# Attention with a two-of-eight expert layer on one core: the attention phase's order, counted in ticks, is replaced by one that is played through

## The chip, the cores and the metric

One NeuronCore of one Trainium2 chip. The time is device microseconds (us) of one execution of the whole program, taken as the median of repeated runs. TensorE is written PE here, VectorE DVE, ScalarE ACT, GpSimd POOL and SyncE SP, as in the profile.

## What is computed

The input is x of 4 batches of 1024 tokens with 512 features, in float32. The output is x + attention(layernorm(x)) + experts(layernorm(x)):

```python
xn = _layernorm(x, axis=-1)
# attention: 16 heads of 32, causal, with a linear distance bias per head
scores = einsum('bhqd,bhkd->bhqk', q, k) / sqrt(D)
scores = where(causal, -inf, scores) + alibi_bias
out = softmax(scores) @ v, then @ Wo.T + bo
# experts: softmax over 8 gates, the two highest per token, weights renormalised
act = silu(g) * u          # g, u = xn @ w1 (352 each)
expert_out = act @ w2
```

## The kernel before

The program has three stretches. A short prologue normalises batch 0 and splits the weights of the attention into float16 pairs (a high and a low half; each product is three float16 products, `PASS`). The **attention phase** follows, and then the **expert phase**, in which 71 slots of 128 gathered tokens each go through one expert's two products and are added to the output by indirect DMAs.

The attention phase is cut into 16 groups (4 batches by 4 groups of 4 heads). A group has 40 **units**, so `NU` is 640. Unit u is one head and one pair of key tiles against two query tiles: PE makes the scores (step `score`, L1271 with L1273, or with L1275 and L1276 on the diagonal) in one of two half banks of PSUM, and ACT takes their exponential (step `exp`, L1875). `score` u waits for `exp` u-2, whose half bank it takes. Four units are a **quad** t, whose exponentials lie in one of three buffers (`PT`). Behind a quad come `add` (POOL sums halves of the exponentials, L1999, L2006, L2010, L2015), `acc` (DVE adds to the row sums, L1656), `pv` (PE, probabilities by values, L1289). `exp` of quad t waits for `pv` and `add` of quad t-3. Behind the quads of a quarter q of the queries come `rsum` (PE, L1299), `osb` (ACT copies the result out of PSUM, L1906), `fold`, `rcp` and `unfold` (a DMA, a reciprocal at L1660 and a DMA back), `bc` (PE, L1309), `a32` (DVE, L1664), `aTh` (ACT, L1855 and L1856) and `aT` (POOL, L2021). `osb` waits for the `aT` that last read the same buffer.

Other work is mixed in between the units:
- for the next group, the q, k and v projections (`qk` L1210, `v` L1227), the copies `qk32` (ACT, L1822), `qkh` (ACT, L1832), `qkl` (POOL, L1984), `vsb` (ACT, L1845) and `stack`, three DMAs for each of 4 heads on SP's queue (L1059);
- for the next group, upper bounds of the scores: 38 pieces `pre` on PE (L1243, L1248), each followed by `mx` on DVE (L1643), then `join`, `mtr` (PE, L1258), `mcp` (ACT, L1882) and the DMA `mrow` (SP, L1076);
- the output projection `o` of a finished batch (PE, L1321, three thirds of four matmuls for each of 8 tiles) with `y` (DVE, L1671) and `ostore`;
- the layer norm of the next batch: `bn` (DVE), `newton` (13 small POOL operations from L1966 on), `xn` (DVE, L1553), `xnh` (ACT, L1778), `xnl` (POOL, L1975), `xtp` (PE, L1165) and `xt` (ACT, L1791);
- the largest magnitude of the experts' weights (`wmax`) and their split into halves (`wsh` ACT L1917, `wsl` DVE L1705, `wstore`), and, from unit 454 on, the routing (`route`, mostly small DVE operations; `slots`, `places`, `lists`).

Four banks of PSUM (`PB`) are lent to `pre`, `qk`, `v`, `o`, `mtr`, `bc` and `xtp` (`borrow`, `give`), and are handed back by the step that empties them: for `pre` that is `mx`.

The order of all this is made by `plan()`, which runs once when the program is built and writes one list of steps. Every engine walks through the list and issues its own steps in that order, each with its waits; so on an engine a step whose wait isn't over holds up all that stand behind it. In the kernel before, `plan()` counts in **ticks**: one tick is one unit. In tick u it writes `score(u)` and `exp(u)`, then whatever is due at fixed distances in ticks (`add` 1 tick behind its quad, `pv` 2, `unfold` 4 and `bc` 9 behind `osb`), up to two `pre` from unit -27 of their group on, one piece of each running job of a list (`pace`), and as much of the projections (`fill`) as a credit allows, which grows by 0.62 of matmul time in each tick. The time that a step takes on DVE, ACT or POOL isn't in this reckoning.

## Time and profile before

| | us |
|---|---|
| median of 3 runs | 1599.39 (1597.41 to 1603.39) |
| the profiled execution, its own time | 1597.73 |
| its span, first to last instruction | 1595.9 |
| first score matmul starts | 74.3 |
| last score matmul starts | 1117.5 |

The profiled execution took 1.83 us more than its span, and 1.66 us less than the median of the runs. The span has the prologue up to 74, the attention phase from 74 to 1118, a turn from 1118 to about 1171 in which the last quarter is finished and the experts' weights are loaded, and the expert phase. On the page, each engine has its busy share; the granted clock of PE stands beside each stretch, 1.00 being 2.4 GHz. A matmul's duration in the trace is longer than what it holds PE for, since matmuls overlap: 0.27 us is shown for one of 256 columns, and the next starts 0.11 us after it.

### The profile page before, as it was taken

To read this page: it belongs to the slowest core of one execution; us is meant where nothing else is said; L and a number is where in the kernel's file an instruction comes from. 1 tells how busy PE (TensorE), PEld (TensorE's weight loads), DVE (VectorE), ACT (ScalarE), POOL (GpSimd) and SP (SyncE) were. 2 spreads that over 40 slices of the span, in tenths; PEclk is the share of its full clock that TensorE was granted. 3 is DMA by queue.
4 is the path that set the end of the run, shared out by engine and by line. 5 is a ranking of instruction groups with operands and counts; after the bars stand their busy time and mean duration, and the time that the engine had idled before them with its cause. 6 is when DMAs were issued, how large, how long until landed. Compare 5 with 4: busy or idle time off the path is not lost.

```text
span 1595.9 us, 32893 instructions
## 1 busy us (share of the span) xinstructions
PE 1419.4 (89%) x12219; PEld 838.9 (53%) x12219; DVE 947.9 (59%) x1742; ACT 799.1 (50%) x1403; POOL 948.4 (59%) x756
## 2 busy tenths in 40 slices
PE   4689978989997999998899899877789999999995
PEld 2355545544554555555455456543356656566663
DVE  8567776666687657766669976672243333333332
ACT  5255666646677675766676455456122222222221
POOL 4134576645577655656675567676217777777774
PEclk9899998989999999998899999997899999999998
DMA  6245433435533536333244210233877778888973
GB/s 245 61 128 148 124 94 102 123 90 148 156 94 97 152 101 197 103 117 94 88 110 126 83 43 13 68 115 106 288 180 126 136 130 131 131 137 148 132 137 47
DMA packets 189156, 193.51 MB, mean 121 GB/s; under 512 B 104883, under 2 KB 138931, under 8 KB 188876
## 3 DMA queue, kind: packets, MB, share of 16 engines
q1 hardware_dynamic: 160492, 152.01, 35.7%
q0 software_dynamic: 26128, 37.24, 13.9%
q8 instruction: 105, 1.72, 0.5%
q10 hardware_dynamic: 2384, 2.16, 0.4%
q14 instruction: 47, 0.39, 0.1%
HBM read 92.88 MB, written 53.74 MB: 92 GB/s over the span
## 4 chain that ended last, share of the span: by engine, by line
PE 55%; DVE 13%; POOL 11%; DMA 7%; issue 6%; ACT 4%; SPq 4%; ACTq 0%; POOLq 0%; DVEq 0%
PE S L1359 15%; PE O L1390 4%; PE M L1390 4%; DVE arena L1643 4%; PE T L1210 3%; DVE arena L1656 3%; DMA arena<-arena 3%; PE M L1289 3%; PE S L1210 3%; PE S L1243 2%; SPq L1059 2%; PE T L1243 2%; PE S L1271 2%; PE O L1289 2%; POOL arena L2006 2%
## 5 line engine op out<-in xcount | busy, mean ns | idle before, releaser
L1875 ACT ACTIVATE arena<-S,psl 128x512 f32<-128x512 f32 (+1 forms) x640 | 399.5, 641 | 256.0 <-PE S L1273 152.2
L2064 POOL DMA_INDIRECT out<-arena x142 | 222.1, 1564 | 104.7 <-issue 40.5
L1359 PE MATMUL S<-arena 128*128 x1704 | 267.1, 313 | 5.2 <-issue 5.2
L1643 DVE TENSOR_REDUCE arena<-S 128x1 f32<-128x512 f32 (+3 forms) x311 | 202.0, 655 | 113.5 <-PE S L1248 82.4
L1643 DVE TENSOR_REDUCE arena<-T 128x1 f32<-128x512 f32 (+3 forms) x297 | 193.0, 654 | 95.5 <-PE T L1248 65.3
L1359 PEld LDWEIGHTS S<-arena 128*128 128x128 f16 x1704 | 166.8, 98 | 102.3 <-issue 5.8
L1271 PE MATMUL S<-arena 106*128 106x256 f16 x640 | 182.0, 285 | 40.7 <-ACT arena L1875 39.2
L1999 POOL TENSOR_TENSOR arena<-arena 128x512 f32<-128x512 f32 (+1 forms) x64 | 135.7, 2121 | 81.5 <-ACT arena L1875 81.4
L1984 POOL TENSOR_TENSOR arena<-arena 128x512 f16<-128x512 f32 x64 | 79.9, 1250 | 165.2 <-ACT arena L1832 165.0
L1763 DVE COPY arena<-T 128x512 f16<-128x512 f16 x71 | 30.1, 425 | 218.4 <-PE T L1374 215.4
L2006 POOL TENSOR_TENSOR arena<-arena 128x1024 f32<-128x1024 f32 x48 | 114.8, 2392 | 75.4 <-ACT arena L1875 46.9
L1243 PE MATMUL S<-arena 105*128 105x512 f16 (+3 forms) x386 | 120.3, 345 | 21.8 <-DVE arena L1643 12.7
L1243 PE MATMUL T<-arena 105*128 105x512 f16 (+3 forms) x382 | 115.8, 342 | 26.4 <-DMA arena<-in_up 10.4
L1928 ACT ACTIVATE arena<-S,sc 128x352 f32<-128x352 f32 x71 | 39.3, 553 | 197.8 <-PE S L1359 197.8
L1656 DVE TENSOR_TENSOR arena<-arena 128x512 f32<-128x512 f32 (+1 forms) x96 | 110.3, 1148 | 36.0 <-POOL arena L2015 19.4
L1271 PEld LDWEIGHTS S<-arena 106*128 106x128 f16 x640 | 64.4, 101 | 103.1 <-ACT arena L1875 61.4
L1210 PE MATMUL T<-arena 128*128 128x512 f16 x420 | 107.8, 384 | 2.4 <-ACT arena L1791 1.0
L1273 PE MATMUL S<-arena 106*128 106x256 f16 x384 | 107.3, 280 | 0.0
L2051 POOL DMA_INDIRECT arena<-xn_d,tl x71 | 73.1, 1030 | 46.3 <-DMA arena<-arena 25.8
L1289 PE MATMUL M<-arena 128*32 128x256 f32 (+1 forms) x1536 | 100.3, 380 | 0.0
L1210 PE MATMUL S<-arena 128*128 128x512 f16 x348 | 92.0, 389 | 3.6 <-DVE arena L1643 3.6
L2010 POOL TENSOR_TENSOR arena<-arena 128x512 f32<-128x512 f32 x48 | 67.9, 1415 | 41.6 <-ACT arena L1875 41.5
(216 smaller groups left out, 2679.4 us busy)
## 6 DMA issues: line engine op xcount, KB each, us to landing
arena<-arena SPq DMA_DIRECT2D x192, 128.0 KB, 3.0
arena<-in_w1T SPq DMA_DIRECT2D x64, 352.0 KB, 3.6
arena<-in_x SPq DMA_DIRECT2D x64, 256.0 KB, 4.2
w_d<-arena SPq DMA_DIRECT2D x32, 352.0 KB, 2.8
arena<-w_d SPq DMA_DIRECT2D x16, 704.0 KB, 6.2
arena<-in_w2T SPq DMA_DIRECT2D x32, 256.0 KB, 3.0
out<-arena SPq DMA_DIRECT2D x32, 256.0 KB, 3.6
xn_d<-arena SPq DMA_DIRECT2D x24, 256.0 KB, 2.8
```

Of the source, the lines that this page charges most:

```text
L1210: tp = pe.matmul(z[:, :], wqkv[:, w_, c, f:f + P], xnT[:, a, c, half * 512:half * 512 + 512], start=(third == 0 and c == 0), stop=(third = ...
L1243: tp = pe.matmul(z[:, n * w:(n + 1) * w], stk[G % 2][0:KROWS - 1, h, 0, j * P:(j + 1) * P], stk[G % 2][0:KROWS - 1, h, 1, k0:k1], start=(n ...
L1271: pe.matmul(z[:, 0:2 * P], K[0], stk[G % 2][0:KROWS, h, 0, q0:q2], start=True, stop=False)
L1289: tp = pe.matmul(YB[o.bank["pv", G, q]][D * x:D * x + D, f:f + n], V[(G + 1) % 3][:, 2 * i + k, x * D:(x + 1) * D], PT[t % 3][:, x, c:c + ...
L1359: tp = pe.matmul(y[:, i * 512:i * 512 + I], xT[:, s % XDEEP, 4 * a + c, :], weights[:, bass.ds(reg[s] + (w_ * NX * W1N + c * 2 * I + i * I ...
L1390: tp = pe.matmul(z[:, :], aTm[0:n, v, 2 * c + a, :], weights[0:n, bass.ds(r2 + (2 * NX * W1N + w_ * NX * W2N + c * E), E)], start=(k == 0) ...
L1643: dve.tensor_reduce(d[:, heads[0]:heads[-1] + 1], z, AX, ALU.max).then_inc(sems["mx"], 1)
L1656: dve.tensor_tensor(AC[q % 2][:, :, f:], AC[q % 2][:, :, f:], z, ALU.add).then_inc(sems["acc"], 1)
L1875: act.activation(PT[t % 3][:, h, 0:n], CB[o.bank["score", u]][:, 0:n], ACT.Exp, scale=psl[:, hh:hh + 1]).then_inc(sems["exp"], 1)
L1999: pool.tensor_tensor(z[:, :, f:f + n], y[:, :, f:f + n], y[:, :, 2 * P:2 * P + n], ALU.add).then_inc(sems["add"], 1)
L2006: pool.tensor_tensor(PSF, y[:, :, 0:2 * P], y[:, :, 2 * P:4 * P], ALU.add).then_inc(sems["add"], 1)
L2064: pool.indirect_dma_start(out=halves, out_offset=bass.IndirectOffsetOnAxis(row[:, part, s:s + 1].bitcast(U32), 0), in_=yo[:, s % YDEEP, c0 ...
```

## The change

The fixed ticks go. Each step of the attention phase is now an object with its engine, a **cost** in us, a **due** number in units, the steps that it follows, an earliest unit (`since`), and the bank that it takes or gives back. `Steps.run` plays them through: at each moment, an engine that is free takes, of the first steps of its lines (a line is all steps of one kind on one engine, in order of their due numbers), the one that is due first among those whose predecessors are done in the play; a step whose predecessors aren't done, or for which no bank is free, is passed over and the engine takes another line's. It is then busy for the step's cost, and the step counts as done after the cost and a lag (0.06 to 0.1 us, 4.2 for a DMA). The order in which the steps are taken in the play is the list. What each step computes, its waits and its buffers are the same; the prologue's list and the expert phase's are the same.

```diff
--- before.py
+++ after.py
+ADD_DUE, ACC_DUE, PV_DUE, RS_DUE = 3, 3.5, 3.2, 6.2
+PRE_DUE, PRE_STEP, MTR_DUE = -27, 1.05, 3.0
+FILL0, FILL1, TURN0, TURN1, STACK_DUE = 4, 38, 6, 44, 0
+LN0, LN_STEP, GATE0 = 55, 18, 120
+O_DUE = (-20, -8, 4, 24)
+MAX_STEP, SPLIT0, SPLIT_STEP = 2.2, 150, 7.4
+PACE = 1.3
...
+DMA_LAG = 4.2
+LAG = {"PE": 0.1, "ACT": 0.06, "DVE": 0.08, "POOL": 0.08, "SP": DMA_LAG}
...
+    def new(self, engine, cost, due, *key, follows=(), line=None, since=None, take=None, give=None, lock=None,
+            sem=None, inc=1, lag=None):
+        s = Step(key, engine, cost, due, list(follows), since, take, give, lock, sem, inc, lag)
+        self.all[key] = s
+        self.lines.setdefault((engine, line or key[0]), []).append(s)
+
+    def run(self, start, pace, last):
+        o, done, free = self.o, {}, dict.fromkeys(LAG, 0.0)
+        lines = {e: [sorted(line, key=lambda s: s.due) for (x, _), line in self.lines.items() if x == e] for e in LAG}
+        left = {e: sum(len(line) for line in lines[e]) for e in LAG}
+        at = {e: [0] * len(lines[e]) for e in LAG}
+        held, tiled, turn, over, pending = None, False, start, None, []
+        t = 0.0
+        given = sorted
+        while any(left.values()):
+            while pending and pending[0][0] <= t + 1e-9:
+                pending.pop(0)[1]()
+            now = turn if turn >= 0 and over is None else (
+                last + (t - over) / pace if over is not None else min(start + t / pace, -0.01))
+            nexts = []
+            for e in LAG:
+                if not left[e]:
+                    continue
+                if free[e] > t + 1e-9:
+                    nexts.append(free[e])
+                    continue
+                best = None
+                for k, line in enumerate(lines[e]):
+                    if at[e][k] == len(line):
+                        continue
+                    s = line[at[e][k]]
+                    if best is not None and s.due >= best[0]:
+                        continue
+                    if s.since is not None and s.since > now:
+                        if turn < 0 or over is not None:
+                            nexts.append(t + (s.since - now) * pace + 1e-6)
+                        continue
+                    if s.lock and held not in (None, s.lock[0]):
+                        continue
+                    if s.take and len(o.owner) == len(o.since):
+                        continue
+                    ready = 0.0
+                    for f in s.follows:
+                        if f in done:
+                            ready = max(ready, done[f])
+                        elif f in self.all:
+                            ready = None
+                            break
+                    if ready is None:
+                        continue
+                    if ready > t + 1e-9:
+                        nexts.append(ready)
+                        continue
+                    best = s.due, k, s
+                if best is None:
+                    continue
+                _, k, s = best
+                at[e][k] += 1
+                left[e] -= 1
+                cost = s.cost
+                if e == "PE":
+                    own = s.key[0] in ("pv", "rsum")
+                    cost += (0.09 if own else 0.13) if own != tiled else 0.0
+                    tiled = own
+                if s.take:
+                    o.borrow(*s.take)
+                kind = s.key[0]
+                if kind == "score":
+                    o.take("C", *s.key)
+                    turn = max(turn, s.key[1])
+                    if s.key[1] == last:
+                        over = t
+                elif kind == "exp":
+                    o.leave("C", ("score", s.key[1]), s.key)
+                elif kind == "pv" and quad(s.key[1])[2] == 0:
+                    o.take("O", "pv", *quad(s.key[1])[:2])
+                elif kind == "osb":
+                    o.leave("O", ("pv", *s.key[1:]), s.key)
+                o.add(*s.key, sem=s.sem, inc=s.inc)
+                if s.lock:
+                    held = None if s.lock[1] else s.lock[0]
+                free[e] = t + cost
+                done[s.key] = t + cost + (LAG[e] if s.lag is None else s.lag)
+                if s.give:
+                    pending.append((done[s.key], lambda s=s: o.give(*s.give)))
+                    pending.sort(key=lambda p: p[0])
+                    nexts.append(done[s.key])
...
-    def score(u):
-        o.take("C", "score", u)
-        add("score", u)
-        add("exp", u)
-        o.leave("C", ("score", u), ("exp", u))
-        if u % 4 == 3:
-            t = u // 4
-            G, q, i = quad(t)
-            at(u + 1, lambda: add("add", t))
-            if i:
-                at(u + 4, lambda: add("acc", t))
-            at(4 * t + 5, lambda: products(t))
-            if t == QUADS - 1:
-                at(4 * t + 9, lambda: sums(t))
...
-        at(now[0] + 4, inverse)
-        at(now[0] + 9, spread)
...
-    due = {}
-    for n in range(len(PIECES) * GROUPS):
-        G, k = divmod(n, len(PIECES))
-        due.setdefault((U0 + k // 2 if k > 2 else U0) if G == 0 else TG * G - 27 + k, []).append(n)
...
-    while u < NU or fill or pace or events or later:
-        now[0] = u
-        flush()
-        if 0 <= u < NU:
-            score(u)
-        for f in events.pop(u, []):
-            f()
-        wanted += due.pop(u, [])
-        for _ in range(2):
-            if wanted and ready.get(("stack", *divmod(wanted[0] // len(PIECES), NG)), u) < u:
-                maxima(wanted.pop(0))
-        if u >= 4 and not (u < 160 * (B - 1) and 70 <= u % 160 < 104):
...
-        credit = min(credit + 0.62, 1.0)
-        for job in list(pace):
-            first, step, steps = job
-            if u >= first and (u - first) % step == 0:
-                cost = next(steps, job)
-                if cost is job:
-                    pace.remove(job)
-                else:
-                    credit -= cost or 0
...
+    for u in range(NU):
+        G, h, q, i = unit(u)
+        t = u // 4
+        b, g = divmod(G, NG)
+        new("PE", 0.22 if i < q else 0.28, u, "score", u,
+            follows=[("exp", u - 2), ("stack", b, g, h), ("mrow", G, q)])
+        new("ACT", 0.63 if i < q else 0.52, u + 0.4, "exp", u, follows=[("score", u), ("pv", t - 3), ("add", t - 3)])
+    for t in range(QUADS):
+        G, q, i = quad(t)
+        b, g = divmod(G, NG)
+        u = 4 * t + 3
+        if i == 0:
+            before = [("rsum", 10 * (G - (q < 2)) + (5, 9, 0, 2)[q])]
+        elif i < q:
+            before = [("acc", t - 1 if i == 2 else t - 3 if q == 3 else t - 6)]
+        else:
+            before = [("acc", t - (3, 3, 4)[q - 1]), ("acc", t - 1) if i > 1 else ("add", t - 1)]
+        new("POOL", (2.2 if q == 0 else 2.35) if i == 0 else 2.35 if i < q else 2.8, u + ADD_DUE, "add", t,
+            follows=[("exp", u), *before])
+        if i:
+            new("DVE", 1.4 if i < q else 0.82, u + ACC_DUE, "acc", t, follows=[("add", t), ("acc", t - 1)][:1 + (i > 1)])
+        new("PE", 0.85 if i < q else 0.64, u + PV_DUE, "pv", t, follows=[
+            ("exp", u), ("vsb", b, g, 1)] + ([("osb", *divmod(4 * G + q - 2, 4))] if i == 0 else []))
+        if i < q:
+            continue
+        d = u + RS_DUE
+        new("PE", 0.43, d, "rsum", t, follows=[("pv", t), ("add", t), ("acc", t)])
+        new("ACT", 0.54, d + 0.8, "osb", G, q, follows=[("rsum", t), ("aT", *divmod(4 * G + q - 2, 4))])
...
+        new("ACT", 0.9, d + 9.5, "aTh", G, q, follows=[("a32", G, q)] + (
+            [("o", b - 1, 2 * q, 2), ("o", b - 1, 2 * q + 1, 2)] if b else []))
+        new("POOL", 0.7, d + 10.5, "aT", G, q, follows=[("aTh", G, q)])
...
+            d = (U0 + k / 2 if k > 2 else U0) if G == 0 else TG * G + PRE_DUE + k * PRE_STEP
+            cost = n / 2400 + 0.0025 * len(heads) + (len(heads) * P / 2400 if k1 == P * (j + 1) else 0)
+            new("PE", cost, d, "pre", G, k, follows=[("stack", b, g, h) for h in heads], take=("pre", G, k))
+            new("DVE", 0.1 + 0.00105 * n, d + 0.6, "mx", G, k, follows=[("pre", G, k), ("mtr", G - 2, q)],
+                give=(("pre", G, k), ("mx", G, k)))
...
+                for third in range(3):
+                    new("PE", 0.87, when(), *key, third, take=key if third == 0 else None, lock=(key, third == 2),
+                        inc=third == 2, since=max(first - 3, U0), line="qkv",
+                        follows=[("xt", b, half, i) for i in range(4)])
...
+        at_ = 160 * (b - 1) + LN0
+        for half in range(2):
+            for i in range(4):
+                before = ("xnl", *((b, 0) if half else (b - 1, 1) if b > 1 else (0, 0)), i)
+                new("SP", 0.6, at_ + (0 if half == 0 else 6 + i), "xload", b, half, i, sem=f"x{i}0", inc=16,
+                    since=at_ - 1 if half == 0 else None, follows=[before], lag=3.0)
+                new("DVE", 0.85, at_ + 4 + 1.2 * i, "bn", b, half, i, follows=[("xload", b, half, i), ("xn", b - 1, half, 3)])
+            new("DVE", 0.45, at_ + 9, "rsq", b, half, follows=[("bn", b, half, 3)])
+            new("POOL", 2.8, at_ + 10, "newton", b, half, follows=[("rsq", b, half)])
+            for i in range(4):
...
+                d = at_ + 12 + 1.3 * i
+                new("DVE", 0.83, d, "xn", b, half, i, follows=[("newton", b, half)])
+                old = half_before(b, half, i)
+                new("ACT", 0.57, d + 0.8, "xnh", b, half, i, follows=[("xn", b, half, i), ("xtp", *old), ("xnd", *old)])
+                new("POOL", 1.3, d + 1.6, "xnl", b, half, i, follows=[("xnh", b, half, i)])
...
+                d, step = at_ + O_DUE[k] + 3 * (i % 2), 0.8
+            key = "o", b, i
+            for third in range(3):
+                new("PE", 0.87, d + step * third, *key, third, take=key if third == 0 else None, lock=(key, third == 2),
+                    inc=third == 2, line="o", since=NU - 1 if b == B - 1 else None,
+                    follows=[("aT", b * NG + g, k) for g in range(NG)] + [("wol", 1)])
...
+    w.run(U0, PACE, NU - 1)
...
```

Two places show what moves. The first is ACT in the second half of the layer norm of batch 2, near unit 257. In the kernel before:

```order
L1875 ACTIVATE arena<-S,psl 128x512 x2
L1855 ACTIVATE arena<-arena,bvs 128x256
L1856 ACTIVATE arena<-arena,bvs 128x256
L1875 ACTIVATE arena<-S,psl 128x512
L1906 ACTIVATE arena<-M 128x512
L1875 ACTIVATE arena<-S,psl 128x512
L1882 ACTIVATE arena<-T 4x256
L1875 ACTIVATE arena<-S,psl 128x384
```

And in the changed kernel (L1806 is `xt`, L1847 `qkh`, L1890 `exp`, L1932 `wsh`, L1870 and L1871 `aTh`, L1897 `mcp`, L1921 `osb`):

```order
L1847 ACTIVATE arena<-arena 128x512
L1890 ACTIVATE arena<-S,psl 128x512
L1932 ACTIVATE arena<-arena,sc 128x704
L1806 ACTIVATE arena<-T 128x8x128
L1870 ACTIVATE arena<-arena,bvs 128x256
L1871 ACTIVATE arena<-arena,bvs 128x256
L1897 ACTIVATE arena<-S 4x256
L1890 ACTIVATE arena<-S,psl 128x512 x3
L1921 ACTIVATE arena<-M 128x512
L1897 ACTIVATE arena<-S 4x256
```

Between `aTh` (L1870, L1871) and the `osb` that needs its `aT` there are now three exponentials and an `mcp`; before there was one exponential. Ahead of this, up to five other steps stand between two exponentials.

The second place is PE at units 166 to 170, where batch 0's output projection falls due. In the kernel before:

```order
L1271 MATMUL S<-arena 128x256
L1273 MATMUL S<-arena 128x256
L1243 MATMUL S<-arena 128x512
L1321 MATMUL S<-arena 128x512 x4
L1271 MATMUL S<-arena 128x256
L1273 MATMUL S<-arena 128x256
L1243 MATMUL T<-arena 128x512
L1248 MATMUL T<-arena 128x128
L1271 MATMUL S<-arena 128x256
L1275 MATMUL S<-arena 128x128
L1276 MATMUL S<-arena 128x2x128
```

And in the changed kernel (L1286, L1288, L1290 and L1291 are `score`, L1225 `qk`, L1258 and L1263 `pre`, L1336 `o`):

```order
L1286 MATMUL S<-arena 128x256
L1288 MATMUL S<-arena 128x256
L1258 MATMUL S<-arena 128x512
L1225 MATMUL T<-arena 128x512 x4
L1336 MATMUL S<-arena 128x512 x12
L1336 MATMUL T<-arena 128x512 x8
L1286 MATMUL S<-arena 128x256
L1290 MATMUL S<-arena 128x128
L1291 MATMUL S<-arena 128x2x128
L1336 MATMUL T<-arena 128x512 x4
```

Where one third of a projection stood between two scores, one of `qk` and five of `o` now do: they fell due before the score of unit 168 and are taken first.

## Rows read from the trace of the kernel before

**Rows 1.** The page: the span, busy time of the engines, and the clock slices.

```profile
span 1595.9 us, 32893 instructions
...
PE 1419.4 (89%) x12219; PEld 838.9 (53%) x12219; DVE 947.9 (59%) x1742; ACT 799.1 (50%) x1403; POOL 948.4 (59%) x756
...
PEclk9899998989999999998899999997899999999998
```

**Rows 2.** Windows: stretch, its length, busy us of PE, PEld, DVE, ACT, POOL, clock.

```profile
74.00:1118.00 1044.00, 934.06 (x9047) 551.46 (x9045) 732.34 (x1273) 645.71 (x1142) 628.67 (x497) 0.95 0.38 108
1040.00:1118.00 78.00, 58.37 (x521) 28.40 (x514) 40.43 (x61) 46.65 (x86) 52.90 (x36) 0.86 0.37 115
1200.00:1560.00 360.00, 360.00 (x2374) 216.62 (x2372) 131.71 (x297) 100.40 (x184) 263.18 (x189) 1.00 0.84 134
```

**Rows 3.** Waits of PE, 74 to 1118: us in total, times, longest.

```profile
PE S L1271 <- ACT arena L1875: 39.2, 32, 4.3
PE S L1243 <- DVE arena L1643: 10.9, 9, 2.9
PE M L1299 <- DVE arena L1656: 7.9, 4, 3.9
PE T L1243 <- DVE arena L1643: 7.1, 5, 3.5
PE S L1258 <- DVE arena L1643: 5.1, 1, 5.1
PE S L1243 <- DVE arena L1664: 4.6, 5, 1.9
PE T L1243 <- ACT arena L1882: 4.3, 4, 1.9
PE S L1243 <- DMA arena<-arena: 3.6, 1, 3.6
```

**Rows 4.** Waits of PE, 1040 to 1118.

```profile
PE S L1271 <- ACT arena L1875: 10.4, 12, 3.4
```

**Rows 5.** Timeline from 499.5: start, us, engine, line, operation, idle before and releaser.

```profile
499.55 0.69 ACT L1875 ACTIVATE arena<-S,psl 128x512 f32<-128x512 f32 x1
...
501.33 2.33 POOL L1999 TENSOR_TENSOR arena<-arena 128x1024 f32<-128x1024 f32 x1
501.34 2.61 DVE L1553 TENSOR_SCALAR arena<-arena,mv,nw 128x512 f32<-128x512 f32 x1
503.63 0.84 POOL L2021 TENSOR_TENSOR arena<-arena 128x256 f16<-128x256 f32 x1
...
504.47 0.53 DVE L1553 TENSOR_SCALAR arena<-arena,mv,nw 128x512 f32<-128x512 f32 x1
504.50 0.60 ACT L1906 ACTIVATE arena<-M 128x512 f32<-128x512 f32 x1 [4.27 <-POOL arena L2021]
...
505.73 0.40 PE L1271 MATMUL S<-arena 106*128 106x256 f16 x1 [4.35 <-ACT arena L1875]
```

**Rows 6.** Timeline, ACT alone, around 235 and 761: `osb` and the idle time before it.

```profile
239.89 0.60 ACT L1906 ACTIVATE arena<-M 128x512 f32<-128x512 f32 x1 [4.21 <-POOL arena L2021]
...
765.92 0.60 ACT L1906 ACTIVATE arena<-M 128x512 f32<-128x512 f32 x1 [4.21 <-POOL arena L2021]
```

**Rows 7.** Windows: three stretches of 58 us, columns as before.

```profile
712.00:770.00 58.00, 49.00 (x469) 29.25 (x470) 40.64 (x71) 35.67 (x65) 38.23 (x49) 0.84 0.24 68
828.00:886.00 58.00, 55.66 (x520) 32.28 (x519) 53.17 (x172) 37.02 (x67) 32.24 (x22) 1.00 0.43 127
886.00:944.00 58.00, 47.60 (x426) 26.70 (x424) 51.27 (x96) 30.08 (x54) 31.98 (x20) 0.94 0.12 37
```

**Rows 8.** One line's instructions, 74 to 1118: shortest, median, longest in ns.

```profile
L1553 DVE TENSOR_SCALAR arena<-arena,mv,nw x24: 495/798/2606, 208.6 to 773.6; 128x512 f32<-128x512 f32 x24
```

**Rows 9.** Groups by form, 74 to 1118: busy us, mean ns.

```profile
L1875 ACT ACTIVATE arena<-S,psl 128x512 f32<-128x512 f32 x384 | 257.5, 685 | 157.5 <-PE S L1273 152.2 <-ACT arena L1882 0.7 <-PE S L1276 0.6
```

**Rows 10.** The chain of waits: one tile of the output projection, 12 matmuls.

```profile
677.91 2.61 PE T L1321 x12
```

**Rows 11.** Timeline, SP's queue: nine DMAs of `stack`.

```profile
1013.87 5.86 SPq L1059 DMA_DIRECT2D arena<-arena  x9
```

More of the change, by code:

```diff
@@ L206, in ln_turn @@
         later.append(rest)
-    def ln_gate(b):
-        while turned.get((b, 1, 3), 1 << 30) >= now[0]:
-            yield 0
-        yield from lock(("gate", b))
-        take_m("gate", b)
-        for part in range(4):
-            add("gate", b, part, inc=part == 3)
-            yield 0.25
-        held[0] = None
-        def rest():
-            add("lg", b)
-            o.give(("gate", b), ("lg", b))
-        later.append(rest)
     def proj_qk(b, g, qk, half):
@@ L271, in plan @@
     ready = {}
-    def stack_when(b, g):
-        while not all(ready.get(("qkl", b, g, qk, half), 1 << 30) <= now[0] for qk in (0, 1) for half in (0, 1)):
-            yield 0
-        while now[0] < TG * (b * NG + g - 1) + 1 and b * NG + g > 1:
-            yield 0
-        for _ in stack(b, g):
-            yield 0
-            yield 0
     def qkv_steps(b, g):
@@ new lines, in plan @@
+    for b in range(1, B):
+        norm(b)
+    for b in range(B):
+        d = 10 if b == 0 else 160 * (b - 1) + GATE0
+        if b == 0:
+            new("ACT", 0.3, 4, "gwh", since=3)
+            new("DVE", 0.95, 4.5, "gwl", follows=[("gwh",)])
+        for part in range(4):
+            key = "gate", b
+            new("PE", 0.7, d + 2 * part, *key, part, take=key if part == 0 else None, lock=(key, part == 3), inc=part == 3,
+                follows=[("xt", b, 1, 3), ("gwl",)])
+        new("DVE", 0.22, d + 8, "lg", b, follows=[("gate", b, 3)], give=(key, ("lg", b)))
@@ L729, in plan @@
-    o.ended, o.forced = u, forced
+                d, step = at_ + O_DUE[k] + 3 * (i % 2), 0.8
[4 more added lines that the diff above has]
+                    follows=[("aT", b * NG + g, k) for g in range(NG)] + [("wol", 1)])
+            new("DVE", 0.7, d + step * 3, "y", b, i, follows=[(*key, 2), ("xbo", b, i)], give=(key, ("y", b, i)))
@@ new lines, in plan @@
+    route(0.95, (0, 0), inc=1)
+    new("ACT", 0.4, d[0] - 1.5, "rex", follows=[("route", 0, 0)])
+    route(1.4, (1, 0), follows=[("rex",)])
+    for i in range(0, NT, 8):
+        route(0.9, (2, i))
+    for i in range(0, NT, 4):
+        route(0.55, (6, i))
+    route(1.4, (10, 0))
+    route(1.1, (11, 0))
+    route(1.5, (11, 1), inc=1)
+    new("PE", 0.9, d[0] - 1.5, "rank", take=("rank",), follows=[("route", 11, 1)])
+    route(0.85, (12, 0), inc=1, follows=[("rank",)])
+    w.all["route", 12, 0].give = ("rank",), ("route", 12, 0)
@@ L731, in up @@
+    for k, (u, n) in enumerate(((603, 10), (622, 4), (NU, 6), (NU, 6), (NU, 2))):
+        new("SP", 0.6 * n, u, "win", k, inc=0, since=u, follows=before + more[k], lag=0.0)
+    w.run(U0, PACE, NU - 1)
     def up(s):
```

425 lines of the change are left out of this document (163 added, 262 removed).

## The prediction

> **What bounds the kernel now.** I read the page first [rows 1]. PE is busy for 89% of the span, DVE, POOL and ACT for 59, 59 and 50%, and the clock slices show full speed with dents. That is an average over stretches with different limits, so I asked for windows next [rows 2]. In the expert phase PE is busy for 360.00 of 360 us at full clock: the order there is the same in both kernels, so nothing is to be gained or lost. In the attention phase, 1044 us from 74 to 1118, PE is busy for 934.1 us, idle for 109.9, and the granted clock is 0.95 in the mean. No other engine is near full (DVE 732, ACT 646, POOL 629 us). So PE bounds this phase, but with gaps. Work at the lower of its two levels (1.2 instead of 2.4 GHz) is done at half rate, so a mean of 0.95 costs 0.05 times 1044, about 52 us. What an order can give back is at most 110 plus 52, or 162 us; it can't take work away, for every step is still there.
>
> The view of PE's waits says what its gaps are [rows 3]. The largest is the score's wait for an exponential, 39.2 us in 32 waits. The next are DVE's: `mx` (L1643), which empties the banks that `pre` and the projections borrow, 10.9 + 7.1 + 5.1 = 23.1 us in the three largest rows (about 29 us with the small ones); `acc` 7.9, `a32` 4.6. The copy `mcp` has 4.3, a DMA 3.6. The rest of the 110 is in waits too short to be named. A wait like these means that the step stood in PE's queue before its input was there, while other work stood behind it.
>
> The timeline shows one such place in full [rows 5]. ACT finishes an exponential at 500.24, then sits idle for 4.27 us in front of `osb` (L1906), whose wait is for `aT` on POOL (L2021). `aT` stands behind a long `add` there, and exponentials that are ready stand behind `osb` on ACT. PE then waits 4.35 us in front of a score. The same wait of 4.2 us stands in two more places, once in each batch's layer norm [rows 6], and the clock falls: 0.84 in the 58 us around the third [rows 7].
>
> **The change, part by part.** The work is the same, so each term is a wait that goes, stays or comes. The sum is made against the profiled execution, 1597.7 us, whose own gaps these are.
>
> 1. `osb` before `aT`. The order now puts three exponentials and an `mcp` between `aTh` and `osb`, where one exponential stood. Three exponentials of 0.685 us [rows 9] cover 2.1 us, against 4.27 in which nothing was done [rows 5], and the layer norm's steps start at unit 55 of each batch instead of 65. Late next is the `add` behind it on POOL. Three stalls of 4.3 us are 13 us; I take 9, between 0 and 13.
> 2. Other waits for an exponential. Of the 39.2 us, 13 are item 1 and 10.4 lie behind 1040 [rows 3, 4]. That leaves 16, made where the old order puts two scores close together while ACT has several copies in its queue. The new play knows both durations. Half, 8 us.
> 3. Waits for `mx`, 29 us. The old order writes a `pre` whether or not DVE has emptied a bank; the new one passes it over while all four banks are out, and takes the next matmul that is ready. This is the wait that the change treats most directly, and DVE is free for 30% of the phase: 17 of 29, between 5 and 25.
> 4. Waits for `acc`, `a32`, `mcp` and the small DVE and ACT rows, some 20 us: 9, between 0 and 15.
> 5. Waits for DMAs. `stack` goes from one head in two units to four heads in about five; each head is three DMAs, and nine of these take SP 5.86 us [rows 11], so 12 take 7.8 and hold up `mrow` and `fold` behind them about as long as before. `unfold` and `mrow` keep their places within two units, except that `mrow` of the third quarter comes at unit 4 instead of -2 in groups 2 and 10; it is needed at 12. The loads for `wmax` end at unit 126 instead of 150, and SP has room. 3 us less, between 5 more and 7 less.
> 6. The last 78 us. The last group has no projections or bounds left to fill PE with, and PE is idle for 19.6 us [rows 2], 10.4 of it for exponentials [rows 4]. No order adds work there. 2 us, between -3 and 8.
> 7. Some 9 us of projections and bounds are now written ahead of the first score. They fill PE while the first row of bounds travels, and are gone later. Nothing, within 5 us either way.
> 8. The turn behind the last score has the same chain of DMAs and the same loads of weights. Nothing, within 5.
>
> The idle time that goes is 9 + 8 + 17 + 9 + 3 + 2 = 48 us. Then the clock: today 52 us are lost beside 110 us of gaps, 0.47 us for each. If the loss follows the gaps, 48 us less of them give back 22 more. Together **70 us**: 1597.7 - 70 = 1527.7. The median of the runs is 1.7 us above this execution, so I forecast **1529 us**, 4.4% less. With all lower bounds at once (0 for items 1, 2 and 4) the sum is a loss of 13 us; with all upper ones (16 for item 2) 94 us of waits go, 138 us with the clock.
>
> One thing the play can't know is that DVE and POOL slow each other. `xn` (L1553) took 2.61 us where it started with POOL's `add`, and 0.53 us right behind [rows 5]; its median is 0.80 and its shortest 0.50 [rows 8], and the play has 0.83. The Trainium skill (Advanced Engine Details and Errata, section VectorE Performance Modes) says that the second SBUF port of VectorE is shared with GpSimd, so that GpSimd instructions and VectorE's two-port modes block each other. By that rule a denser phase has more such meetings, and speaks against the change; the two rows of `xn` agree with it. Since the median of `xn` is at the play's value, I leave the sum as it is; the rows bound it at 24 times (2.61 - 0.83), 43 us of DVE's time, most of which PE would not see.
>
> **Rivals.**
> - **DVE takes over.** Where the routing runs, from 828 to 944, DVE is busy for 53.17 + 51.27 of 116 us, 90% [rows 7]. PE still has gaps there, but no order makes room on DVE. If a phase 70 us shorter (DVE 732 of 974, 75%) also brings stretches like this at the layer norms, where `bn`, `xn`, `wmax` and `mx` meet, items 3 and 4 give 6 instead of 26, and item 1 gives 5: 24 us, with the clock 35. 1597.7 - 35 + 1.7 = 1564. Against it stands the mean load.
> - **The clock comes back whole.** The clock is 1.00 in stretches in which PE is busy for 55.7 of 58 us [rows 7]. If gaps long enough to bring it down are just those that go, the gain is 48 + 52 = 100 us, 1499. The Trainium skill (TensorE: Matmul & The Clock Gate, Part 1) says that the low level is the default and that activity releases it, which would make the time this. Against it: the low clock of the last 78 us, 0.86 [rows 2], stays in any order. All gaps and all of the clock would give 1437, which I leave out.
> - **Slower: exponentials starve behind bursts.** The play takes what is due first, and work that was held up and is overdue goes ahead of a score. At unit 168 six thirds of projections stand between two scores, where there was one; a tile's three thirds take 2.61 us [rows 10], so that is 5.2 us. Reckoned from such durations, over 3 us of other matmuls stand between two scores at 25 places of the new order, 4.0 us in the mean, against 9 before. Meanwhile ACT has two half banks of scores, 2 x 0.685 us of work [rows 9], and idles for the other 2.6. If each of the 16 further places is paid for, because ACT then has 4 us to catch up and PE has spent the work that would fill that time, that is 42 us and 20 more by the clock, less the 48 that items 1 to 6 give: 14 us slower, 1613. It decides once PE's own wait behind a burst is above about 2 us on average. Against it: ACT is busy for 646 of 1044 us, and a bank of ready work is due most of the time.
> - **Nothing comes of it.** The waits change places: the step taken instead is itself early by as much, since half the chain runs through POOL and DMAs whose times vary. 1592 to 1607. That the order isn't changed at all is excluded by the listing.
>
> **How the numbers follow.** My forecast, with 1510 to 1550 around it, has a chance of 0.45; DVE takes over 0.18; the clock whole 0.17; nothing 0.08; slower 0.12. A measurement can tell about 0.5%, 8 us. The first three are faster by more than that, 0.80 together. The range from **1475 to 1594** leaves out the slower case, most of nothing, and the far end of the clock's.
>
> **What would show it.** Right: between the first and the last score some 970 us instead of 1044, PE idle for about 62 in it and a clock near 0.97; no wait of 4 us in front of `osb`; waits for `mx` at a third. The scores' wait for exponentials should fall least. Wrong: PE idle for 100 us or more in it, with long rows of scores waiting for exponentials (bursts), or DVE above 85% (DVE takes over). The expert phase should be the same to a few us; if the time moves there, my split of the program is wrong.

## The result, and the profile after

The changed kernel takes 1512.16 us (1509.29 to 1514.04, 4 runs); the kernel before took 1601.39 us in the runs beside it. The ratio is 0.9442, with a 95% interval from 0.9412 to 0.9472: 5.6% faster, 89 us. The forecast was 1529 us, 4.4%. The profiled execution has a span of 1511.8 us, 84.1 less than before. Of the ten runs of the kernel called "the three stalls alone" below, one took 1719.72 us at a clock of 0.824, and its ratio leaves that run out.

The page of the changed kernel, with the lines that answer to [rows 1]:

```profile
span 1511.8 us, 32885 instructions
...
PE 1397.8 (92%) x12219; PEld 822.2 (54%) x12219; DVE 982.6 (65%) x1742; ACT 807.1 (53%) x1403; POOL 941.7 (62%) x756
...
PEclk9899999999999999999999999989899999999998
```

The number of instructions on each engine is the same. The dents in the clock's slices are nearly gone from the attention phase. The windows, answering to [rows 2] (stretch, its length, busy us of PE, PEld, DVE, ACT, POOL, clock); the first is from the first score to the last:

```profile
82.10:1033.10 951.00, 902.43 (x8928) 526.21 (x8927) 762.38 (x1269) 647.67 (x1132) 617.22 (x493) 0.99 0.40 115
956.00:1034.00 78.00, 66.58 (x635) 33.32 (x635) 48.00 (x77) 52.56 (x97) 61.74 (x42) 0.93 0.40 127
1116.00:1476.00 360.00, 360.00 (x2377) 216.79 (x2376) 131.45 (x296) 100.66 (x185) 263.20 (x189) 1.00 0.87 134
```

The same stretch of the kernel before, from the first score to the last:

```profile
74.30:1117.50 1043.20, 933.26 (x9043) 550.91 (x9042) 731.68 (x1273) 645.43 (x1141) 628.67 (x497) 0.95 0.38 108
```

So it goes from 1043.2 to 951.0 us, 92.2 less. Split by PE: idle time falls from 109.9 to 48.6 us (-61.3), busy time from 933.3 to 902.4 (-30.9). The first score starts 7.8 us later (82.1 instead of 74.3). -61.3 - 30.9 + 7.8 = -84.4; from the last score to the end it is 478.7 us against 478.4, 0.3 more, and so the span's difference is 84.1. The expert phase is unchanged.

Not all of the 30.9 us is a gain. Some matmuls now stand ahead of the first score. This stretch, before and then after:

```profile
0.00:74.30 74.30, 39.69 (x283) 22.88 (x284) 48.54 (x100) 32.66 (x41) 22.91 (x45) 0.89 0.49 157
0.00:82.10 82.10, 49.74 (x396) 31.20 (x397) 50.94 (x102) 37.49 (x48) 26.42 (x48) 0.92 0.58 181
```

These are 113 matmuls and 10.0 us of PE's time, which leaves 21 of the 30.9. The pages say the same: for the same 12219 matmuls PE was busy for 1419.4 us and is for 1397.8, 21.6 less.

PE's waits in the phase, answering to [rows 3] (us in total, times, longest; all lines after the twelfth are under 1 us). Line numbers of the changed kernel are higher by 15: L1286 is `score`, L1258 `pre`, L1658 `mx`, L1314 `rsum`, L1671 `acc`, L1273 `mtr`, L1663 `join`.

```profile
PE S L1286 <- ACT arena L1890: 11.8, 22, 2.2
PE M L1314 <- DVE arena L1671: 8.9, 8, 3.2
PE S L1273 <- DVE arena L1663: 3.4, 2, 2.1
PE S L1258 <- DVE arena L1658: 3.1, 3, 1.6
PE T L1258 <- DVE arena L1658: 3.0, 4, 1.4
PE T L1324 <- DVE arena L1658: 2.8, 1, 2.8
PE T L1273 <- DVE arena L1663: 2.2, 3, 0.8
```

The score's wait for an exponential is 11.8 us instead of 39.2, and the longest 2.2 instead of 4.3. All waits for `mx` together are 13 us instead of 29. No wait for a DMA is left. The wait for `acc` is as long as before (9.7 us in its two rows against 9.0), and one for `join` is new.

### The profile page after: what moved, and what is told of

Its sections match the earlier page's. It is cut to its first block, busy times and chain, and to the rows that moved or that the text cites. A ratio compares the mean times of both kernels' runs of the same rounds, so it can differ in the third digit from the quotient of the medians.

```text
span 1511.8 us, 32885 instructions
## 1 busy us (share of the span) xinstructions
PE 1397.8 (92%) x12219; PEld 822.2 (54%) x12219; DVE 982.6 (65%) x1742; ACT 807.1 (53%) x1403; POOL 941.7 (62%) x756
## 4 chain that ended last, share of the span: by engine, by line
PE 69%; DVE 13%; POOL 6%; DMA 4%; issue 4%; ACT 2%; SPq 2%; ACTq 0%; POOLq 0%; DVEq 0%
PE S L1374 16%; PE O L1405 4%; PE M L1405 4%; PE T L1225 4%; PE M L1304 4%; DVE arena L1658 4%; PE S L1225 4%; PE S L1286 3%; PE S L1336 3%; PE T L1258 3%; PE S L1258 3%; PE O L1304 3%; PE T L1242 2%; PE S L1288 2%; DVE arena L1671 2%
## 5 line engine op out<-in xcount | busy, mean ns | idle before, releaser
L1890 ACT ACTIVATE arena<-S,psl 128x512 f32<-128x512 f32 (+1 forms) x640 | 393.4, 642 | 181.4 <-PE S L1288 93.5
L1658 DVE TENSOR_REDUCE arena<-T 128x1 f32<-128x512 f32 (+3 forms) x312 | 199.8, 651 | 64.9 <-PE T L1263 48.6
L1658 DVE TENSOR_REDUCE arena<-S 128x1 f32<-128x512 f32 (+3 forms) x296 | 191.0, 655 | 41.1 <-PE S L1263 27.7
L1286 PE MATMUL S<-arena 106*128 106x256 f16 x640 | 176.5, 277 | 12.6 <-ACT arena L1890 11.8
L1778 DVE COPY arena<-T 128x512 f16<-128x512 f16 x71 | 30.2, 425 | 217.7 <-PE T L1389 205.5
L1671 DVE TENSOR_TENSOR arena<-arena 128x512 f32<-128x512 f32 (+1 forms) x96 | 122.4, 1275 | 24.8 <-POOL arena L2030 16.9
L1258 PE MATMUL T<-arena 105*128 105x512 f16 (+3 forms) x405 | 116.0, 326 | 15.9 <-DMA arena<-in_up 10.4
L1999 POOL TENSOR_TENSOR arena<-arena 128x512 f16<-128x512 f32 x64 | 79.6, 1244 | 58.4 <-ACT arena L1847 58.3
L1258 PE MATMUL S<-arena 105*128 105x512 f16 (+3 forms) x363 | 109.3, 334 | 5.1 <-DVE arena L1658 3.1
L1225 PE MATMUL T<-arena 128*128 128x512 f16 x432 | 111.1, 385 | 0.9 <-DVE arena L1603 0.6
L2036 POOL TENSOR_TENSOR arena<-arena 128x256 f16<-128x256 f32 x64 | 48.7, 761 | 100.3 <-ACT arena L1871 100.3
L1286 PEld LDWEIGHTS S<-arena 106*128 106x128 f16 x640 | 62.8, 98 | 79.3 <-ACT arena L1890 37.3
L1288 PE MATMUL S<-arena 106*128 106x256 f16 x384 | 104.5, 274 | 0.0
```

Source lines behind the costliest of these rows:

```text
L1225: tp = pe.matmul(z[:, :], wqkv[:, w_, c, f:f + P], xnT[:, a, c, half * 512:half * 512 + 512], start=(third == 0 and c == 0), stop=(third = ...
L1258: tp = pe.matmul(z[:, n * w:(n + 1) * w], stk[G % 2][0:KROWS - 1, h, 0, j * P:(j + 1) * P], stk[G % 2][0:KROWS - 1, h, 1, k0:k1], start=(n ...
L1286: pe.matmul(z[:, 0:2 * P], K[0], stk[G % 2][0:KROWS, h, 0, q0:q2], start=True, stop=False)
L1288: tp = pe.matmul(z[:, 2 * P:4 * P], K[1], stk[G % 2][0:KROWS, h, 0, q0:q2], start=False, stop=True)
L1658: dve.tensor_reduce(d[:, heads[0]:heads[-1] + 1], z, AX, ALU.max).then_inc(sems["mx"], 1)
L1671: dve.tensor_tensor(AC[q % 2][:, :, f:], AC[q % 2][:, :, f:], z, ALU.add).then_inc(sems["acc"], 1)
```

## Experiments

All are compared by the ratio to the kernel before that ran beside them; the changed kernel's is 0.9442.

**Is it the durations?** The play with every cost and lag outside PE at 0.05 us, so that the order follows the due numbers alone:

```diff
+        if engine != "PE":
+            cost, lag = 0.05, 0.05
         s = Step(key, engine, cost, due, list(follows), since, take, give, lock, sem, inc, lag)
```

> The changed kernel with every cost and lag outside PE set to 0.05 us in the play, so that the order follows the due numbers alone. Theory A (the gain comes from knowing the durations of ACT, DVE, POOL and the DMAs): the waits come back, 1575 us or more against 1512 of the changed kernel and 1600 of the one before. Theory B (the new due numbers make the gain, the durations little): 1530 us or less. Between them both count.

Measured: 2251.57 us, ratio 1.407 (1.3972 to 1.4167). Theory A, far beyond its bound: the new due numbers alone don't give an order that is worse by a few waits, but one that is 740 us slower than the changed kernel. A step that seems ready at once is written right behind its predecessor, and then it blocks its engine for the whole latency. Some 300 of the 740 us lie ahead of the first score, which starts at 379.9 us instead of 82.1; from the first to the last score it is 1398.6 us instead of 951.0. In the play the weights' loads land at once, so all 56 steps of `wmax` and most of the split (L1722 is `wsl` here) were written ahead of the first score, and DVE, busy for only 135 us of that stretch, waits in them while `mx` stands behind:

```profile
0.00:379.90 379.90, 68.79 (x400) 36.57 (x401) 135.35 (x219) 75.11 (x94) 27.00 (x49) 0.58 0.53 160
```

```profile
L1722 DVE SCALAR_TENSOR_TENSOR arena<-arena,sc 128x704 f16<-128x704 f32 (+2 forms) x46 | 41.0, 890 | 161.3 <-ACT arena L1934 161.3
```

PE's waits in the whole run (`mx` is L1660 here):

```profile
PE T L1260 <- DVE arena L1660: 153.0, 46, 28.1
PE T L1227 <- DVE arena L1660: 94.6, 6, 67.0
```

and ACT's, where a piece of the weights' split (L1934 is `wsh`) is written right behind the store of the piece before it:

```profile
ACT arena L1934 <- DMA w_d<-arena: 196.9, 55, 9.8
```

**DMAs or engines?** The same for ACT, DVE and POOL, with SP's costs and the DMA lags kept.

```diff
+        if engine in ("ACT", "DVE", "POOL") and lag != DMA_LAG:
+            cost, lag = 0.05, 0.05
```

> The changed kernel with cost and lag of ACT, DVE and POOL at 0.05 us in the play; PE's costs and all DMA lags kept. The flat play lost 740 us. Theory C (most of that is DMAs, whose 4.2 us of lag keeps bc, rcp and score from being written too early): the time comes down to 1540 to 1640. Theory D (the three engines' durations made that loss): above 1800.

Measured: 1834.33 us, ratio 1.1487 (1.146 to 1.1514). Theory D's number, but the two split the loss: of the 740 us, 417 go with the DMAs' costs and lags and 322 stay with the engines. The 417 are no price of DMA latencies alone: the first score is back at 86.6 us, so 293 of them are the late start of the run before, and no run leaves out the DMAs' latencies with the engines' durations kept. DVE's waits show where (L1673 is `acc`, L2023 and L2032 are forms of `add`):

```profile
DVE arena L1673 <- POOL arena L2023: 143.7, 43, 11.0
DVE arena L1673 <- POOL arena L2032: 141.2, 48, 5.2
```

**One engine at a time.** ACT, then POOL, then DVE, then of DVE's steps `mx` alone. The edit takes in the few DMAs that ACT and POOL issue themselves (on ACT `fold`, `unfold` and `mrow` of the last group), whose lags the run with all three mostly kept.

```diff
+        if engine == "ACT":
+            cost, lag = 0.05, 0.05
```

> The changed kernel with ACT's costs alone at 0.05 us in the play. The largest wait of the kernel before was a score's for its exponential (39 us, 12 now). If knowing ACT's time is what removed it, 30 us or more above 1512; if scores and exponentials keep their distance by the due numbers, within 10 us.

Measured: 1583.0 us, ratio 0.9903 (0.9882 to 0.9923), 71 us above the changed kernel. PE's waits for exponentials are back in good part, 29.4 us against 11.8 (L1288 is `score`):

```profile
PE S L1288 <- ACT arena L1892: 29.4, 54, 3.6
```

That is 18 of the 71 us; the others are spread over small waits for ACT's copies, 7 us of waits for DMAs in the last group, and a PE that is busy for 28 us longer between the scores.

POOL, with the same edit:

> The changed kernel with POOL's costs alone at 0.05 us in the play. With ACT, DVE and POOL all so, DVE waited 285 us for add. If that comes from acc being written right behind an add that takes 2.4 us on POOL, 1700 us or more; if it takes DVE's own durations to go wrong too, below 1650.

Measured: 1584.85 us, ratio 0.9906 (0.9878 to 0.9933), 73 us. The second answer: DVE waits for `add` 84.5 + 59.2 us in this run, half of the 285 with all three, but that costs 73 us and not the 188 or more of the first answer.

```profile
DVE arena L1673 <- POOL arena L2023: 84.5, 39, 11.4
...
DVE arena L1673 <- POOL arena L2032: 59.2, 31, 7.6
```

DVE, with the same edit:

> The changed kernel with DVE's costs alone at 0.05 us in the play. With mx alone it was 45 us slower, with POOL alone 73, with ACT alone 71, with all three 322. If the losses of single engines add, DVE's own is 150 us or more (1660); if they multiply, since each wrong order hides the readiness of the next engine, it is 45 to 90 us (1557 to 1600).

Measured: 1649.73 us, ratio 1.0295 (1.0257 to 1.0334), 138 us above the changed kernel and slower than the kernel before. It lies between my two numbers, nearer to the one for losses that add: 71 + 73 + 138 = 282 against the 322 with all three. Its PE waits are mainly those for `mx`, over 70 us in all rows, beside 23.4 us for exponentials. The three largest for `mx`:

```profile
PE S L1260 <- DVE arena L1660: 22.2, 20, 5.2
PE T L1260 <- DVE arena L1660: 20.4, 21, 5.6
PE S L1227 <- DVE arena L1660: 14.2, 3, 9.0
```

`mx` alone:

```diff
-            new("DVE", 0.1 + 0.00105 * n, d + 0.6, "mx", G, k, follows=[("pre", G, k), ("mtr", G - 2, q)],
+            new("DVE", 0.05, d + 0.6, "mx", G, k, follows=[("pre", G, k), ("mtr", G - 2, q)],
```

> The changed kernel with the cost of mx alone at 0.05 us in the play: banks seem free at once. If passing over a pre without a bank is what removed the waits for mx (29 us before, 13 now), they come back, and the time is 15 to 25 us above 1512. If the order of pre and mx is set by the due numbers anyway, within 5 us.

Measured: 1557.28 us, ratio 0.9736 (0.9683 to 0.9789), 45 us, twice what I expected. The waits did come back:

```profile
PE S L1258 <- DVE arena L1658: 11.4, 13, 2.4
PE M L1314 <- DVE arena L1671: 10.0, 8, 3.2
PE T L1258 <- DVE arena L1658: 5.5, 13, 1.3
```

All of PE's rows for `mx` sum to 38 us against 13. PE's idle time between the scores, by the window below, is 78.1 us against 48.6, and its busy time 917.8 against 902.4, at a clock of 0.97. So 25 us of named waits stand for 45 us of time: some 5 of other gaps and 15 of a slower PE come with them.

```profile
83.30:1079.20 995.90, 917.77 (x8924) 530.63 (x8922) 758.04 (x1268) 649.36 (x1135) 615.79 (x493) 0.97 0.38 110
```

**Or the due numbers?** The play with all its costs, and the old distances in ticks as due numbers for `add`, `acc`, `pv`, the bounds, the layer norm and the output projection. Those of the q, k and v projections, of `stack` and of the experts' weights stay as in the changed kernel.

```diff
-ADD_DUE, ACC_DUE, PV_DUE, RS_DUE = 3, 3.5, 3.2, 6.2
-PRE_DUE, PRE_STEP, MTR_DUE = -27, 1.05, 3.0
-LN0, LN_STEP, GATE0 = 55, 18, 120
-O_DUE = (-20, -8, 4, 24)
+ADD_DUE, ACC_DUE, PV_DUE, RS_DUE = 1, 4, 2, 6.2
+PRE_DUE, PRE_STEP, MTR_DUE = -27, 1.0, 3.0
+LN0, LN_STEP, GATE0 = 65, 21, 108
+O_DUE = (-6, 2, 11, 44)
```

> The changed kernel, played with all its costs, but with the old tick distances as due numbers (add 1, pv 2, acc 4, layer norm from 65, the output projection at -6, 2, 11, 44). Theory A (the play makes the gain): within 15 us of 1512. Theory B (the new due numbers make it): 1550 or more.

Measured: 1524.55 us, ratio 0.9541 (0.9523 to 0.9559), 12 us above the changed kernel. Theory A: with these old dues the play still has 73 of the 89 us.

**The three stalls alone.** In the kernel before, `osb` and the chain behind it come three ticks later, in the three places of [rows 5, 6], which takes `osb`'s wait out:

```diff
-        at(now[0] + 1, lambda: emptied(G, q))
+        at(now[0] + (4 if q == 1 and G in (2, 6, 10) else 1), lambda: emptied(G, q))
```

> The kernel before, with osb of quarter 1 in groups 2, 6 and 10 three ticks later, past the exponentials that stood behind it. If the three stalls of 4.3 us are worth their own size and the clock's, 13 to 18 us less than the kernel before (1584 to 1587). If the wait is only passed on to POOL's add, less than 5 us.

Measured: 1595.03 us, ratio 0.9957 (0.993 to 0.9984): 3 to 11 us faster by the interval, 7 in its middle. That is less than 13 to 18 and not clearly more than 5, so in the main the wait is passed on. `osb`'s waits for `aT` fall from 14.1 us to 1.4, but the timeline of ACT and then of POOL at the same place shows what is late next:

```profile
497.42 0.58 ACT L1875 ACTIVATE arena<-S,psl 128x384 f32<-128x384 f32 x1 [0.17 <-PE S L1276]
500.13 0.63 ACT L1778 ACTIVATE arena<-arena 128x512 f16<-128x512 f32 x1 [2.13 <-DVE arena L1553]
```

```profile
497.45 2.36 POOL L1999 TENSOR_TENSOR arena<-arena 128x1024 f32<-128x1024 f32 x1
499.77 0.85 POOL L2021 TENSOR_TENSOR arena<-arena 128x256 f16<-128x256 f32 x1
```

ACT now sits in front of `xnh` (L1778), whose `xn` (L1553) is the DVE operation that stretches beside POOL's `add`. Half of the stall was passed on to it.

**Bursts between scores.** The scores are due five units earlier, so that overdue projections would no longer go ahead of them.

```diff
-        new("PE", 0.22 if i < q else 0.28, u, "score", u,
+        new("PE", 0.22 if i < q else 0.28, u - 5, "score", u,
```

> The changed kernel with each score due five units earlier, so that no overdue projection goes ahead of a score whose exponential buffer is free. If the bursts between scores starve ACT and cost time, 10 us or more below the changed kernel's 1512. If they are harmless, within 5 us of it, or slower, since PE then spends its scores early and has them no longer when a bank is missing.

Measured: 1509.51 us, ratio 0.9427 (0.9377 to 0.9477): no difference from the changed kernel that these runs can tell. But the edit didn't do what it was made for. Counted in the traces, over 3 us of other matmuls stand between two scores at 29 places of the changed kernel, 5.8 us at most, and at 28 places here, 6.3 us at most; such a place of this run, with all six thirds of two tiles (L1336) ahead of a score:

```profile
298.67 1.03 PE L1225 MATMUL T<-arena 128*128 128x512 f16 x4
299.53 2.75 PE L1336 MATMUL T<-arena 128*128 128x512 f16 x12
302.12 2.75 PE L1336 MATMUL S<-arena 128*128 128x512 f16 x12
304.71 0.27 PE L1286 MATMUL S<-arena 106*128 106x256 f16 x1
```

So this run says nothing of the price of bursts, and no run was made without them. The changed kernel's own trace says something. One of its longest bursts, 5.4 us from 330.97, leaves ACT idle for 3.2 us, yet PE is busy for all but 0.02 us of the 56 us around it:

```profile
306.00:362.00 56.00, 55.98 (x490) 31.16 (x489) 40.68 (x60) 38.39 (x65) 30.79 (x22) 1.00 0.52 157
```

The window from first to last score of the run with earlier scores also shows that the work written ahead of the first score is a mere shift: here the first score starts at 74.8 as in the kernel before, and the last is at 1029.9 instead of 1033.1.

```profile
74.80:1029.90 955.10, 909.61 (x9014) 532.35 (x9011) 768.25 (x1276) 648.06 (x1137) 618.39 (x494) 0.98 0.41 116
```

**Can the play be made truer?** A shorter DMA lag. The 2.4 us is the median of the 128 KB DMAs of `stack`; the same constant stands for `fold`, `unfold` and `mrow`, of which the page has no median, and the loads keep their own 2.5 to 3.5 us.

```diff
-DMA_LAG = 4.2
+DMA_LAG = 2.4
```

> The changed kernel with a DMA lag of 2.4 us in the play instead of 4.2, the traced median from issue to landing. PE has no wait for a DMA left. If 4.2 holds slack that costs nothing, the time stays within 5 us of 1512; if it is what a busy queue needs, steps behind fold and unfold come too early and it is 10 us or more slower.

Measured: 1503.4 us, ratio 0.9409 (0.9383 to 0.9435). It isn't slower, and 9 us below the changed kernel rather than within 5; the interval overlaps the changed kernel's, so a gain of its own isn't shown. With the scores' earlier due as well:

> The changed kernel with the DMA lag at 2.4 us and the scores due five units earlier. Each alone gave 1503 and 1510 against 1512. If they add, 1498 to 1502; if the lag alone is what helps, 1503.

Measured: 1495.56 us, ratio 0.9346 (0.9322 to 0.937). This lies wholly below the changed kernel's interval: a further 1%, the fastest of all, and somewhat below the 1498 to 1502 that I gave for two gains that add. And the lag with `xn` at its duration beside POOL:

```diff
-                new("DVE", 0.83, d, "xn", b, half, i, follows=[("newton", b, half)])
+                new("DVE", 1.4, d, "xn", b, half, i, follows=[("newton", b, half)])
```

> As the run with the lag of 2.4 us, and with xn at 1.4 us in the play, its traced median beside POOL in the changed kernel, where the play had 0.83. If DVE's meetings with POOL make the play wrong where it counts, 3 us or more below 1503; if DVE has room for them, within 2 us.

Measured: 1504.72 us, ratio 0.9406 (0.938 to 0.943), the same as with the lag alone: the play was wrong about `xn`, and it didn't matter.

## Why the prediction was right, point by point

The direction, the mechanism and the place were right: PE's gaps in the attention phase closed by more than half, the expert phase didn't move, and the run lies in the range. It was 17 us too cautious. By the steps of the sum:

- *The bound.* PE, with gaps. The runs agree: the idle time that went is 61 us, against the 48 forecast.
- *Item 1, `osb`.* No score waits over 2.2 us any more, so the 13 us are gone from PE's waits, where 9 were forecast. `osb` itself waits for `aT` for 2.9 us in all, against 14.1:

```profile
ACT arena L1921 <- POOL arena L2036: 2.9, 4, 1.3
```

  By time, the 9 us and 4 more of clock were too much for the stalls alone: the run that takes out only them gains some 7. At the same place of the changed kernel ACT keeps working, though 8 us earlier it is idle for 1.9 us in front of `xnh`, for `xn`:

```profile
464.84 0.71 ACT L1890 ACTIVATE arena<-S,psl 128x512 f32<-128x512 f32 x1
465.41 0.90 ACT L1932 ACTIVATE arena<-arena,sc 128x704 f16<-128x704 f32 x1
466.60 1.02 ACT L1806 ACTIVATE arena<-T 128x1024 f16<-128x1024 f16 x1 [0.28 <-PE T L1180]
...
470.85 0.69 ACT L1890 ACTIVATE arena<-S,psl 128x512 f32<-128x512 f32 x1 [1.04 <-PE S L1288]
471.44 0.59 ACT L1921 ACTIVATE arena<-M 128x512 f32<-128x512 f32 x1
```

- *Item 2, other exponentials.* 39.2 - 13 - 10.4 = 16 us before, 11.8 - 5.4 = 6.4 now (the last 78 us have 5.4). That is 10 us less, and 8 were forecast. I had expected this wait to fall least; it fell most, from 39.2 to 11.8 in all.
- *Item 3, `mx`.* 29 to 13 us, 16 against 17 forecast.
- *Item 4.* Mis-sized. The rows for `mcp` are gone (5.9 us) and those for `a32` went from 6.0 to 1.3, but `acc` is at 9.7 us against 9.0, and `join` has 5.6 that weren't there: from 21 to 17, 4 us instead of 9. All rows that are neither for an exponential nor for `mx` or a DMA, those of the layer norm too, went from 31 to 22. `acc` follows an `add` of 2.4 us on POOL that itself follows an exponential; that this chain is no shorter in another order is a reading, which no run tests.
- *Item 5, DMAs.* 7 us of waits before, none now; 3 forecast.
- *Item 6, the last 78 us.* Mis-sized, and its reason was wrong: 8 us instead of 2. PE's idle time there went from 19.6 to 11.4 us. I argued that no order adds work there, but the stretch now holds 71 units instead of 62, and with them 19 matmuls of `lists` and `o` where there were none; PE is busy for 66.6 us instead of 58.4. By PE's waits, those of the scores went from 10.4 to 5.4 us and those for `acc` from 8.4 to 2.6, and `join` has 2.9. So what closed were waits between ACT, POOL, DVE and PE; no run was made for it.
- *Items 7 and 8.* In sum as forecast, the turn equal and the first score 7.8 us later. But the 10 us of work ahead of it fill little idle time: PE is idle there for 32.4 us instead of 34.6. The work is only moved.
- *The clock.* PE's busy time fell by 21 us for the same work, against the 22 forecast, but this agreement is partly luck. The step was that the loss follows the gaps, 0.47 us for each; with 61 us of gaps gone it gives 29, and the low clock went faster than the gaps. Over the stretches of the phase at the lower level, first of the kernel before, then of the changed one, the length and PE's busy time sum to

```profile
sum 106.88, PE 93.52; mean PE 4.07
sum 23.91, PE 22.45; mean PE 4.49
```

  The low level took 107 us and takes 24, 78% less, while the gaps shrank by 56%. By the mean clock (0.95, now 0.99) some 42 us should have come back. Low-clock time that fell into gaps explains little of the difference to 21: PE was busy for 93.5 of the 106.9 us. At half rate, 71 us less of busy low time are up to 35 us. Why PE's busy time fell by 21 only stays open; a short wait inside a matmul's shown duration counts as busy too, and may have grown.

Of the rivals, DVE is busy for 762 of 951 us, 80%, and 89% in the two windows with the routing, and PE is idle for only 1.1 and 6.0 us in them:

```profile
754.00:810.00 56.00, 54.95 (x497) 31.41 (x496) 52.80 (x165) 36.19 (x64) 29.14 (x19) 1.00 0.27 84
810.00:866.00 56.00, 49.98 (x395) 26.18 (x394) 47.29 (x94) 29.20 (x53) 28.44 (x23) 0.94 0.20 53
```

DVE doesn't take over, but it is the engine whose durations the play needs most (138 us). The clock did come back nearly whole, as that rival said, and in the last 78 us too, where the forecast had its 0.86 stay: it is 0.93. The rival's 1499 was 13 us too low, as it took all 52 us for that, of which 21 came, while 13 us more of gaps went than forecast. The slower rival didn't come: over 3 us of other matmuls stand between two scores at 29 places, and the scores' wait for exponentials is still 11.8 us in all, since PE has other ready work. Its sum was also uneven, 20 us of clock for the new waits and none for the 48 us of old ones; with those 22 it is 8 us faster than the kernel before, not 14 slower. On the port, `xn` has a median of 1.375 us now against 0.798 [rows 8]:

```profile
L1568 DVE TENSOR_SCALAR arena<-arena,mv,nw x24: 529/1375/2681, 176.0 to 700.5; 128x512 f32<-128x512 f32 x24
```

Five of the 24 take more than 2.6 us. Each of them starts within 0.04 us of a 128x1024 `add` on POOL and ends 0.28 us behind its end; the two that meet no POOL operation take 0.53 us, and so do five that start 0.2 to 0.5 us ahead of one. One of the five begins the row of four `xn` on DVE here:

```profile
697.03 2.35 POOL L2014 TENSOR_TENSOR arena<-arena 128x1024 f32<-128x1024 f32 x1
```

```profile
696.99 4.89 DVE L1568 TENSOR_SCALAR arena<-arena,mv,nw 128x512 f32<-128x512 f32 x4 [0.17 <-POOL nw L1985]
```

The Trainium skill (Advanced Engine Details and Errata, section VectorE Performance Modes) says that VectorE's second SBUF port is shared with GpSimd, so that GpSimd instructions and VectorE's two-port modes block each other; these rows agree. That a denser phase has more such meetings was the prediction's own step, and the higher median bears it out. What these meetings cost isn't shown: the run with `xn` at 1.4 us tells only that a play that knows of them gains nothing.

What stays open: why the shorter lag and the earlier scores give 1% together when neither shows a gain of its own outside its interval, how much of the 45 us of `mx` is the clock, why PE's busy time gave back only half of what the clock's mean says, and what the bursts cost. None was taken further.

## What to carry to other kernels

Where engines run in order and one list feeds them all, write the list by playing it through with durations read from a trace; fixed distances cost over 5% here. The durations needn't be exact (0.83 for 1.4 us did nothing, 4.2 for 2.4 us of DMA little), but they have to be there for every engine: leaving out one engine's cost 71 to 138 us, leaving out the three engines' 322, and the DMAs' costs and latencies beside them 417 more, most of it ahead of the first score. When you price a removed stall, look for the step that is late next: here the three stalls gave back about half of their size (7 us of 13, or 3 to 11 by the interval). When you price the clock, compare PE's busy time for the same work, and not the mean clock alone. And when a run is made to take something out, count in its trace whether it is out: the run against the bursts kept them all.

## What was not expected of the hardware

When the mean granted clock between the first and the last score rose from 0.95 to 0.99, PE's busy time for the same work fell by about 21 us, where the means say 42; gaps are no more than a small part of the reason. And a `tensor_scalar` of 128x512 on DVE takes from 0.5 to 2.7 us by what POOL does beside it, five times its own length, while POOL's `add` of 128x1024 beside it took its usual 2.33 to 2.36 us.
